# Two-layer kernel: order and size of loads at the borders of projection, scan and mix

## The chip, the cores and the metric

The kernel runs on one core of a Trainium2 chip. The metric is the device time of one execution in microseconds. TensorE multiplies matrices, VectorE and ScalarE do elementwise work, GpSimd does elementwise work and small tables, and SyncE (SP) issues DMAs; ScalarE issues some too. Each engine runs its own list of instructions in order, and semaphores tie the lists together.

## The reference

Two layers on x of 2 x 4096 tokens with 512 channels, all in float32. Biases are added where a matrix is applied. In the names of the kernel:

```
xn  = layernorm(x)
z   = silu(depthwise_conv3(xn @ w1.T + b1))             # over tokens
y   = ssm(z)         # h = h * sigmoid(A) + z * B; y = sum(h * C) + D * z, 16 states a channel
v   = silu(xn @ v1.T + bv1)
x2  = x + (y * v) @ w2.T + b2 + mxfp6(xn) @ mxfp6(Wf).T + bf
xn2 = layernorm(x2)
out = x2 + linear_attention_norm(xn2) + rwkv_channel_mix(xn2)
```

`mxfp6` scales blocks of 32 values by their largest magnitude over 7.5 and rounds to a grid of six-bit numbers. The recurrence of `ssm` runs over the 4096 tokens of a sequence; the kernel takes it in chunks of 16 tokens, with a small convolution inside a chunk and a scan from chunk to chunk. The linear attention needs sums over all tokens of a sequence of k, and of k times v, before its first output.

## The kernel before, in words

The first layer is one block of three phases that run into each other: `phase_project`, `phase_scan`, `phase_mix`. `run_phases` gives each engine the list of the three phases one after the other. The second layer follows in a block of its own. All orders are written out by hand.

**Projection.** 16 groups g of 512 tokens. VectorE normalises group g + 1 in `body(g)` (`normalise`, L285 to L302: statistics, rstd from GpSimd, then four scalings of 128x512). TensorE transposes it (`turn_x`, L486) between the products of group g, which are three products a piece (`split_products`, L99 to L101). ScalarE takes the x1 banks (L439) and the v banks (L452), and the centre tap of the convolution; VectorE adds the side taps (`side_terms`, L322 and L325), then takes the low part of the transposed x (`low_part`, L307), for which the turn of channel tile kt + 2 waits. VectorE also prepares tables of the scan at the end of a body: `state_rates` at g = 1 and 2, `state_powers` at g = 3 (four doublings, a last product, a copy, and a memset of `kpad`, L363), `kernel_rows` at g = 5. GpSimd raises the state matrix to powers by `power_bit(j)` behind the rstd of groups 4 to 7. SP stores z and v of each group; in the last group it stores v and z of channel tile 0, of tile 1, and of tiles 2 and 3. z of tile 0 of the last two units counts on `z_head`.

**Scan.** 64 steps o, eight channels each. SP loads z of a step into one of Z = 6 buffers (L592). TensorE makes three matmuls a step, of two passes each: `own` (L747) one step ahead, `toep` (L765), `outof` (L768). VectorE runs the recurrence (`scan`, L629) from `own` to `outof`. ScalarE takes y (L699) and stores it from one of Y = 4 buffers (L703). GpSimd expands three tables a step (L611). In between stand other jobs, by step number:

```
    TURN_AT, WEIGHTS_AT, QUANTISE_AT = 24, 32, 8
    MIX_IN_AT, MIX_PREPARE_AT, MIX_TURN_AT, MIX_HEAD_AT = 42, 44, 60, 61
```

VectorE quantises Wf in nine steps from QUANTISE_AT. ScalarE's queue loads Wf (`wf_nat`, 1 MB) before step 0 (L710), and at step 4 w2, Wk and Wv, 1 MB each, and three bias rows (L719 to L722). Two x tiles are normalised (`normalise_input`) and quantised (`prepare_step`, seven steps each; `finish_quantising` on GpSimd at 56 and 63); tile 0 is turned at 60.

**Mix.** 64 tiles N of 128 tokens, and pairs of tiles. Each tile takes a bank that ScalarE fills with the biases (`set_sums`, L996), quantised x times Wf and gated y times w2. VectorE adds x and takes statistics (`sums`, L1131), then ScalarE normalises and keys follow a tile or two later. The gated pair is `gate` (L1073, VectorE, once y and v are loaded), `high_u` (L974, ScalarE), `low_u` (L939, GpSimd). In iteration N, VectorE does `prepare_step(N + 2, ...)` and every second time a gate before `sums(N)`; GpSimd does `low_u` of the next pair after tile N's rstd when N is odd.

## Time and profile before

| | |
|---|---|
| median of 3 runs | 2188.6 us (2184.38 to 2189.14) |
| the profiled execution's own time | 2185.81 us |
| its span | 2184.0 us |
| mean granted TensorE clock | 0.986 |
| TensorE busy | 2108.4 us, 97% of the span |
| VectorE busy | 1509.2 us, 69% |
| ScalarE busy | 1058.5 us, 48% |
| GpSimd busy | 826.6 us, 38% |

Times within the trace count from the span's start. Busy time is what an engine's instructions take; a matmul's end is modelled, so that matmuls overlap in the record and their starts are what tells the pace. Idle time ahead of an instruction stands in brackets with what released it. The granted clock (PEclk) is TensorE's, 1.00 for its full 2.4 GHz.

### The profile page before, as it was taken

What the parts mean: (1) busy time and instruction counts of PE and PEld (TensorE: products, weight loads), DVE (VectorE), ACT (ScalarE), POOL (GpSimd) and SP (SyncE); (2) the same over time, 40 slices, a digit from 0 to 9 for tenths busy, and PEclk for the clock granted to TensorE, in tenths of its full rate; (3) what the DMA queues carried; (4) which work ended last, traced back from release to release, by engine and by line L of the source; (5) the groups of instructions that cost most, each with busy time, mean ns of one, the idle gap of its engine ahead of it and who ended that gap; (6) DMA issues with size and microseconds to landing.
All of it is one profiled execution on the core that took longest, in us unless ns stands there. A gap on an engine that the chain in (4) does not pass through costs nothing. (4 is left out here: it accounts for less than half of the span.)

```text
span 2184.0 us, 27599 instructions
## 1 busy us (share of the span) xinstructions
PE 2108.4 (97%) x9466; PEld 1671.5 (77%) x9466; DVE 1509.2 (69%) x2949; ACT 1058.5 (48%) x1770; POOL 826.6 (38%) x843
## 2 busy tenths in 40 slices
PE   7999999899899999999999999599999999999998
PEld 6878888534478888888888887478888888888887
DVE  4776655466577777776777774377777777777777
ACT  4545555323255555555555554355554444555443
POOL 1021000254445454444454453034434444443444
PEclk9999999999989999999999999799999999999999
DMA  4333533666533333332343331412222122222211
GB/s 148 125 112 133 162 121 107 237 216 211 183 106 126 97 116 117 106 116 97 118 143 106 108 125 49 145 49 87 85 80 68 68 68 87 87 85 80 68 39 39
DMA packets 173493, 241.38 MB, mean 111 GB/s; under 512 B 18857, under 2 KB 109225, under 8 KB 172202
## 3 DMA queue, kind: packets, MB, share of 16 engines
q1 hardware_dynamic: 161576, 216.10, 29.8%
q10 hardware_dynamic: 11778, 23.53, 2.9%
q8 instruction: 75, 1.23, 0.2%
q14 instruction: 64, 0.52, 0.1%
HBM read 138.86 MB, written 100.73 MB: 110 GB/s over the span
## 5 line engine op out<-in xcount | busy, mean ns | idle before, releaser
L99 PE MATMUL bank<-e_ring,e_w_hi 128*128 128x512 f32 x512 | 204.4, 399 | 22.2 <-DVE e_ring L1571 16.7
L1236 PE MATMUL bank<-d_kh,d_nat 128*128 128x512 f32 x768 | 196.0, 404 | 5.5 <-DVE d_kh L1122 5.5
L100 PE MATMUL bank<-e_ring,e_w_hi 128*128 128x512 f32 x512 | 200.6, 392 | 0.0
L101 PE MATMUL bank<-e_ring,e_w_lo 128*128 128x512 f32 x512 | 200.3, 391 | 0.0
L1571 DVE TENSOR_TENSOR e_ring<-e_mixed,e_ring 128x512 fp32r<-128x512 f32 x128 | 96.0, 750 | 122.6 <-ACT e_ring L1469 122.6
L1500 ACT ACTIVATE e_kr<-bank 128x512 f32<-128x512 f32 x64 | 38.0, 593 | 289.9 <-PE bank L101 233.0
L957 POOL TENSOR_TENSOR rstd<-d_var_eps,neg_half 128x1 f32<-128x1 f32 x64 | 35.3, 551 | 359.7 <-DVE d_var_eps L1142 359.7
L1236 PEld LDWEIGHTS bank<-d_kh,d_nat 128*128 128x128 f32 x768 | 141.3, 191 | 35.4 <-issue 6.5
L1450 POOL TENSOR_TENSOR e_x<-e_x,e_beta 128x512 f32<-128x512 f32 x64 | 82.9, 1295 | 223.8 <-ACT e_y L1491 223.8
L1430 POOL TENSOR_TENSOR e_x<-e_x,e_ff 128x512 f32<-128x512 f32 x64 | 83.2, 1301 | 196.3 <-DVE e_ff L1632 196.3
L247 POOL TENSOR_TENSOR b_rstd<-b_var_eps,neg_half 128x4 f32<-128x4 f32 x16 | 16.2, 1012 | 318.4 <-DVE b_var_eps L296 318.4
L99 PEld LDWEIGHTS bank<-e_ring,e_w_hi 128*128 128x128 f32 x512 | 96.7, 189 | 50.5 <-DVE e_ring L1571 18.9
L1021 ACT ACTIVATE d_xt<-bank 128x512 f32<-128x512 f32 x64 | 38.4, 599 | 190.8 <-PE bank L1199 190.8
L629 DVE TENSOR_TENSOR_SCAN c_state<-decay,bank 128x255 f32<-128x255 f32 x128 | 80.5, 670 | 71.4 <-PE bank L747 71.4
L1564 DVE SCALAR_TENSOR_TENSOR e_mixed<-e_xt,cols,e_prev 128x512 f32<-128x512 f32 x128 | 102.9, 804 | 20.3 <-ACT e_prev L1478 19.8
L307 DVE TENSOR_TENSOR b_xt<-bank,b_xt 128x512 fp32r<-128x512 f32 x64 | 44.0, 690 | 104.9 <-ACT b_xt L402 104.6
L101 PEld LDWEIGHTS bank<-e_ring,e_w_lo 128*128 128x128 f32 x512 | 96.8, 189 | 20.6
L1434 POOL TENSOR_TENSOR e_y<-e_y,e_att 128x512 f32<-128x512 f32 x64 | 107.0, 1671 | 14.3 <-DVE e_att L1651 14.3
L99 PE MATMUL bank<-d_w,d_ut 128*128 128x512 f32 x256 | 102.3, 400 | 10.1 <-POOL d_ut L939 5.6
L100 PEld LDWEIGHTS bank<-e_ring,e_w_hi 128*128 128x128 f32 x512 | 96.9, 189 | 18.8
L1147 DVE TENSOR_TENSOR d_nat<-d_xn,d_nat 128x512 fp32r<-128x512 f32 x64 | 78.2, 1222 | 47.2 <-ACT d_nat L1038 47.2
L99 PE MATMUL bank<-d_wk,d_nt 128*128 128x512 f32 x256 | 105.2, 411 | 0.0
(209 smaller groups left out, 6364.6 us busy)
## 6 DMA issues: line engine op xcount, KB each, us to landing
scr_v<-b_vt SPq DMA_DIRECT2D x64, 256.0 KB, 2.7
scr_z<-b_zt SPq DMA_DIRECT2D x64, 256.0 KB, 2.1
c_z<-scr_z SPq DMA_DIRECT2D x64, 256.0 KB, 2.7
scr_y<-c_y ACTq DMA_DIRECT2D x64, 256.0 KB, 2.7
d_x<-in_L_attn_x SPq DMA_DIRECT2D x64, 256.0 KB, 3.5
scr_x<-d_x SPq DMA_DIRECT2D x64, 256.0 KB, 2.1
scr_xnt<-d_xt SPq DMA_DIRECT2D x32, 512.0 KB, 4.0
e_xt<-scr_xnt SPq DMA_DIRECT2D x16, 1024.0 KB, 5.7
```

The lines of the kernel that those rows point to most:

```text
L99: eng.matmul(out, lhs[hi], rhs[hi], start=first, stop=False, skip_group_check=onto)
L100: eng.matmul(out, lhs[hi], rhs[lo], start=False, stop=False, skip_group_check=onto)
L101: return eng.matmul(out, lhs[lo], rhs[hi], start=False, stop=last, skip_group_check=onto)
L307: nc.vector.tensor_tensor(xt[g % 2][:, 1, kt, :], TB[kt % 2][:, :], xt[g % 2][:, 0, kt, :].bitcast(F32), ALU.subtract).then_inc(lo_done, 1)
L629: nc.vector.tensor_tensor_scan(state[o % 2][:, b, 1:], rate, SB[o % 2][:, b * NCB:(b + 1) * NCB - 1], 0.0, ALU.mult, ALU.add).then_inc(sta ...
L1147: nc.vector.tensor_tensor(nat[q][:, 1, :], xn[N % 2][:, :], nat[q][:, 0, :].bitcast(F32), ALU.subtract).then_inc(nat_lo, 1)
L1236: mm = pe.matmul(BG[c][:, :], s[:, i, cols], r[:, j, :], start=M % NTB == 0 and i == j, stop=M % NTB == NTB - 1 and i == 1, skip_group_che ...
L1430: nc.gpsimd.tensor_tensor(x2[h][:, t, :], x2[h][:, t, :], ff[t % 2][:, :], ALU.add).then_inc(base_done, 1)
L1434: nc.gpsimd.tensor_tensor(y[t][:, :], y[t][:, :], att[t % 2][:, :], ALU.add).then_inc(sum_done, 1)
L1450: nc.gpsimd.tensor_tensor(x2[h][:, t, :], x2[h][:, t, :], beta[:, :], ALU.add).then_inc(shifted, 1)
L1564: nc.vector.scalar_tensor_tensor(mixed[kt % 2][:, :], current(g % 2, kt), mu[:, kt:kt + 1], prev[kt % 2][:, :], ALU.mult, ALU.add).then_in ...
L1571: nc.vector.tensor_tensor(ring[slot][:, 1, kt, :], src, ring[slot][:, 0, kt, :].bitcast(F32), ALU.subtract).then_inc(lo_done, 1)
```

## The change

Where each load, table and tile stands in the engines' queues:

- Projection: `state_powers` is done in two parts, three doublings at g = 3 and the last with the rest at g = 4. The memset of `kpad` goes to GpSimd, ahead of everything. `kernel_rows`, its matmuls, and the store and the eight loads of the table go one group later. GpSimd's `power_bit` waits until its group has been normalised.
- SP loads the first six z blocks (`load_first_z`) behind the z stores of channel tile 1 of the last group, ahead of v and z of tiles 2 and 3.
- ScalarE's queue loads Wf in four pieces of 256 KB at steps 1 to 4, w2, Wk and Wv in twelve at every second step from 6 to 28, the bias rows at 30, 32 and 34. Quantising Wf starts at step 10, not 8. `join_biases` goes from step 24 to 42.
- Three x tiles, not two, are normalised and quantised in the scan, from step 38 and 40 on; tile 0 is turned at 56 and its high and low parts are taken at 57 and 58. In the mix, pair 1's `high_u` and `low_u` come ahead of tile 1, and iteration 0 quantises no tile.

```diff
@@ phase_project, sync
                     store_v(g, parts_v)
                     for c in units_in(g):
                         store_z(c, parts_z)
+                    if parts_z == (1,):
+                        keep["load_first_z"]()
                 continue
...
-            if g == 6:
+            if g == 7:
                 sp.wait_ge(k_step, 3)
...
-            if g == 7:
+            if g == 8:
                 sp.wait_ge(kern_out, 16)
@@ phase_project, gpsimd
+        nc.gpsimd.memset(kpad[:, :, :], 0.0).then_inc(keep["set"], 1)
...
             if g in (4, 5, 6, 7):
+                pool.wait_ge(xn_done, GT * (g + 1))
                 power_bit(g - 4)
@@ phase_project, vector
-        def state_powers():
-            for j in range(4):
+        def state_powers(doublings):
+            for j in doublings:
...
+            if 3 not in doublings:
+                return
...
-            nc.vector.memset(kpad[:, :, :], 0.0).then_inc(a_step, 1)
...
-            if g == 5:
+            if g == 6:
                 kernel_rows()
...
-            if g == 3:
-                state_powers()
+            if g in (3, 4):
+                state_powers(range(3) if g == 3 else (3,))
@@ phase_project, tensor
-            if g == 4:
+            if g == 5:
                 pe.wait_ge(a_step, 14)
@@ phase_scan
-    TURN_AT, WEIGHTS_AT, QUANTISE_AT = 24, 32, 8
-    MIX_IN_AT, MIX_PREPARE_AT, MIX_TURN_AT, MIX_HEAD_AT = 42, 44, 60, 61
+    TURN_AT, WEIGHTS_AT, QUANTISE_AT = 24, 32, 10
+    QUANTISED_AT, WEIGHT_PIECES_AT, BIASES_AT = 1, 6, 30
+    MIX_IN_AT, MIX_PREPARE_AT, MIX_BANKS_AT, MIX_TURN_AT, MIX_HEAD_AT = 38, 40, 42, 56, 61
+    MIX_FINISH_AT = {50: 0, 57: 1, NO - 1: 2}
...
+    def load_z(o):
+        nc.sync.dma_start(zo[o % Z][:, :], z_of[o]).then_inc(z_in[o % Z], 16)
+
+    def load_first_z():
+
+        nc.sync.wait_ge(*project["turned"])
+        nc.sync.wait_ge(*project["x1"])
+        nc.sync.wait_ge(*project["z_head"])
+        for h in range(2):
+            nc.sync.wait_ge(*project["z_front"][h])
+        for o in range(Z):
+            load_z(o)
...
@@ phase_scan, sync
+        project["store_last_v"]()
+        for o in range(Z, NO):
             if o == NO // KT:
                 for h in range(2):
                     sp.wait_ge(*project["z"][h])
-            if o >= Z:
-                sp.wait_ge(y_full, o - Z + 1)
-            sp.dma_start(zo[o % Z][:, :], z_of[o]).then_inc(z_in[o % Z], 16)
-            if o == 3:
-                project["store_last_v"]()
+            sp.wait_ge(y_full, o - Z + 1)
+            load_z(o)
@@ phase_scan, gpsimd
-            if o == 24:
+            if o == MIX_BANKS_AT:
                 mix["join_biases"]()
-            if o in (56, NO - 1):
-                mix["finish_quantising"](0 if o == 56 else 1)
+            if o in MIX_FINISH_AT:
+                mix["finish_quantising"](MIX_FINISH_AT[o])
@@ phase_scan, vector
-            if MIX_PREPARE_AT <= o < MIX_PREPARE_AT + 2 * mix["steps"]:
+            if MIX_PREPARE_AT <= o < MIX_PREPARE_AT + 3 * mix["steps"]:
                 mix["prepare_step"](*divmod(o - MIX_PREPARE_AT, mix["steps"]))
+            if o == MIX_TURN_AT + 2:
+                mix["low_q"](0)
...
-            if o == NO - 1:
-                mix["low_q"](0)
@@ phase_scan, scalar
-        act.dma_start(wf_nat[:, :].rearrange("p (t k) -> p t k", t=KT),
-                      ins["L0_ffn_weight"].rearrange("(t p) k -> p t k", p=P)).then_inc(wf_in, 16)
...
+            if QUANTISED_AT <= o < QUANTISED_AT + KT:
+                t = o - QUANTISED_AT
+                act.dma_start(wf_nat[:, t * D:(t + 1) * D], ins["L0_ffn_weight"][t * P:(t + 1) * P, :])\
+                   .then_inc(wf_in, 16)
...
-                act.dma_start(w2_raw[:, :, :], ins["L0_attn_w2_w"]).then_inc(raw_in[0], 16)
-                act.dma_start(wk_raw[:, :, :], ins["L1_attn_Wk"]).then_inc(raw_in[1], 16)
-                act.dma_start(wv[:, :, :], ins["L1_attn_Wv"]).then_inc(late["wv_in"], 16)
-                mix["load_biases"]()
+            if WEIGHT_PIECES_AT <= o < WEIGHT_PIECES_AT + 2 * 3 * KT and (o - WEIGHT_PIECES_AT) % 2 == 0:
+                i, kt = divmod((o - WEIGHT_PIECES_AT) // 2, KT)
+                tile, name, done = pieces[i]
+                act.dma_start(tile[:, kt, :], ins[name][:, kt, :]).then_inc(done, 16)
+            if o in (BIASES_AT, BIASES_AT + 2, BIASES_AT + 4):
+                mix["load_bias"]((o - BIASES_AT) // 2)
...
-            if o in (MIX_IN_AT, MIX_IN_AT + 1):
+            if MIX_IN_AT <= o < MIX_IN_AT + 3:
                 mix["normalise_input"](o - MIX_IN_AT)
...
-            if o == NO - 2:
+            if o == MIX_TURN_AT + 1:
                 mix["high_q"](0)
@@ phase_mix, gpsimd
-            if N % 2 and N // 2 + 1 < NT // 2:
+            if (N % 2 or N == 0) and N != 1 and N // 2 + 1 < NT // 2:
                 low_u(N // 2 + 1)
-            if N + 2 < NT:
+            if N and N + 2 < NT:
                 finish_quantising(N + 2)
@@ phase_mix, scalar
         high_u(0, BEHIND)
-        normalise_input(2)
+        high_u(1)
...
-            if N % 2 and N // 2 + 1 < NT // 2:
+            if N % 2 and N > 1 and N // 2 + 1 < NT // 2:
                 high_u(N // 2 + 1)
@@ phase_mix, vector
-            if N + 2 < NT:
+            if N and N + 2 < NT:
                 for k in range(PREP):
                     prepare_step(N + 2, k)
```

## Rows read from the trace of the kernel before

**Rows 1.** Timeline, ScalarE: start us, us, instruction, [idle before <- releaser].

```profile
114.78 0.69 ACT L439 ACTIVATE b_ring<-bank,cols 128x512 f32<-128x512 f32 x1 [1.08 <-PE bank L101]
...
146.49 0.69 ACT L439 ACTIVATE b_ring<-bank,cols 128x512 f32<-128x512 f32 x1 [3.08 <-PE bank L101]
...
170.18 0.69 ACT L439 ACTIVATE b_ring<-bank,cols 128x512 f32<-128x512 f32 x1 [1.06 <-PE bank L101]
```

**Rows 2.** Windows: busy us (instructions) of each engine, PEclk, DMA share, GB/s.

```profile
120.00:130.00 10.00, 6.95 (x30) 5.57 (x29) 8.83 (x16) 3.38 (x6) 7.00 (x4) 0.89 0.10 39
614.40:619.20 4.80, 4.78 (x11) 3.79 (x12) 4.59 (x8) 0.00 (x0) 2.62 (x2) 0.50 0.16 60
```

**Rows 3.** Timeline, VectorE, in the projection.

```profile
116.35 1.76 DVE L363 MEMSET b_kpad<- 8x2048 f32 x1 [0.36 <-issue]
...
123.96 4.66 DVE L302 TENSOR_SCALAR b_xg<-b_xg,b_moments,b_rstd 128x512 f32<-128x512 f32 x4
...
196.64 1.91 DVE L302 TENSOR_SCALAR b_xg<-b_xg,b_moments,b_rstd 128x512 f32<-128x512 f32 x4
...
206.28 0.68 DVE L307 TENSOR_TENSOR b_xt<-bank,b_xt 128x512 fp32r<-128x512 f32 x1
```

**Rows 4.** Timeline, TensorE, projection and scan.

```profile
210.96 0.60 PE L486 MATMUL bank<-consts,b_xg 128*128 128x128 f32 x4
...
410.13 3.78 PE L747 MATMUL bank<-c_z,c_into 128*128 128x512 f32 x4 [7.72 <-DMA c_z<-scr_z]
...
415.83 1.02 PE L747 MATMUL bank<-c_z,c_into 128*128 128x512 f32 x2
...
439.00 1.02 PE L747 MATMUL bank<-c_z,c_into 128*128 128x512 f32 x2
...
446.80 1.91 PE L747 MATMUL bank<-c_z,c_into 128*128 128x512 f32 x2
...
470.42 1.02 PE L747 MATMUL bank<-c_z,c_into 128*128 128x512 f32 x2
```

**Rows 5.** DMA issues (x, KB, us to landing): all; 403.6-404; 425-445; 592.3-592.7.

```profile
c_z<-scr_z SPq DMA_DIRECT2D x64, 256.0 KB, 2.7
...
c_z<-scr_z SPq DMA_DIRECT2D x1, 256.0 KB, 6.5
...
d_wv<-in_L_attn_Wv ACTq DMA_DIRECT2D x1, 1024.0 KB, 10.3
...
d_v<-scr_v SPq DMA_DIRECT2D x1, 512.0 KB, 4.6
```

**Rows 6.** Timeline, ScalarE, in the scan.

```profile
443.55 0.60 ACT L699 ACTIVATE c_y<-bank 128x512 f32<-128x512 f32 x1 [8.90 <-DMA scr_y<-c_y]
```

**Rows 7.** Timeline, TensorE, start of the mix.

```profile
601.29 0.80 PE L99 MATMUL bank<-d_w,d_ut 128*128 128x512 f32 x1 [4.47 <-ACT bank L996]
...
614.42 0.76 PE L99 MATMUL bank<-d_w,d_ut 128*128 128x512 f32 x1 [4.46 <-POOL d_ut L939]
...
625.94 0.39 PE L99 MATMUL bank<-d_w,d_ut 128*128 128x512 f32 x1
```

**Rows 8.** Timeline, SyncE, end of the projection.

```profile
396.22 0.91 SPq L213 DMA_DIRECT2D scr_z<-b_zt  x2
...
398.25 0.94 SPq L213 DMA_DIRECT2D scr_z<-b_zt  x2
```

**Rows 9.** Timeline, VectorE, start of the mix.

```profile
598.78 1.22 DVE L1073 TENSOR_TENSOR d_ut_raw<-d_ut_raw,d_v 128x1024 f32<-128x1024 f32 x1
599.92 0.68 DVE L1131 TENSOR_TENSOR d_x<-bank,d_x 128x512 f32<-128x512 f32 x1
```

**Rows 10.** Timeline, ScalarE, start of the mix.

```profile
604.94 1.04 ACT L974 ACTIVATE d_ut<-d_ut_raw 128x1024 fp32r<-128x1024 f32 x1
...
610.53 0.61 ACT L996 ACTIVATE bank<-d_res_bias 128x512 f32<-128x512 f32 x1
```

**Rows 11.** Timeline, GpSimd, start of the mix.

```profile
611.92 2.35 POOL L939 TENSOR_TENSOR d_ut<-d_ut_raw,d_ut 128x1024 fp32r<-128x1024 f32 x1
```

More of the change, by code:

```diff
@@ L362, in state_powers @@
             nc.vector.tensor_copy(keep["decay"][:, :], a_cs[:, 4, :]).then_inc(a_step, 1)
-            nc.vector.memset(kpad[:, :, :], 0.0).then_inc(a_step, 1)
         def kernel_rows():
-            dve.wait_ge(a_step, 17)
+            dve.wait_ge(a_step, 16)
+            dve.wait_ge(keep["set"], 2)
             for i in range(2):
@@ L577, in phase_scan @@
     }
-    def sync(sp):
-        sp.wait_ge(*project["turned"])
-        sp.wait_ge(*project["z_head"])
-        for h in range(2):
-            sp.wait_ge(*project["z_front"][h])
-        for o in range(NO):
-            if o == 3:
-                sp.wait_ge(*project["x1"])
+    def load_z(o):
[8 more added lines that the diff above has]
+            load_z(o)
+    keep["load_first_z"] = load_first_z
+    def sync(sp):
+        project["store_last_v"]()
+        for o in range(Z, NO):
             if o == NO // KT:
@@ L643, in quantise_step @@
         def quantise_step(k):
-            dve.wait_ge(wf_in, 16)
+            dve.wait_ge(wf_in, 16 * KT)
             if k:
@@ L706, in weight_high @@
             if kt == 0:
-                act.wait_ge(raw_in[i], 16)
+                act.wait_ge(raw_in[i], 16 * KT)
             nc.scalar.activation(tile[:, 0, kt, :], raw[:, kt, :], ACT.Copy).then_inc(w_hi, 1)
-        act.dma_start(wf_nat[:, :].rearrange("p (t k) -> p t k", t=KT),
-                      ins["L0_ffn_weight"].rearrange("(t p) k -> p t k", p=P)).then_inc(wf_in, 16)
+        pieces = [(w2_raw, "L0_attn_w2_w", raw_in[0]), (wk_raw, "L1_attn_Wk", raw_in[1]),
+                  (wv, "L1_attn_Wv", late["wv_in"])]
         for o in range(NO):
             take(o)
-            if o == 4:
+            if QUANTISED_AT <= o < QUANTISED_AT + KT:
+                t = o - QUANTISED_AT
+                act.dma_start(wf_nat[:, t * D:(t + 1) * D], ins["L0_ffn_weight"][t * P:(t + 1) * P, :])\
+                   .then_inc(wf_in, 16)
+            if o == WEIGHT_PIECES_AT:
                 for h in range(2):
@@ L730, in scalar @@
             store(o)
[L731 removed]
+            if MIX_IN_AT <= o < MIX_IN_AT + 3:
                 mix["normalise_input"](o - MIX_IN_AT)
[L733 removed]
+            if o == MIX_BANKS_AT + 6:
                 mix["set_sums"](0)
@@ L771, in tensor @@
                 turn_weight(o - TURN_AT)
-            if o == MIX_IN_AT:
+            if o == MIX_BANKS_AT:
                 mix["open_banks"]()
@@ L961, in gpsimd, with load_bias @@
                                         -1.0, ALU.mult, ALU.mult).then_inc(norm_done, 1)
-            if N % 2 and N // 2 + 1 < NT // 2:
+            if (N % 2 or N == 0) and N != 1 and N // 2 + 1 < NT // 2:
                 low_u(N // 2 + 1)
-            if N + 2 < NT:
+            if N and N + 2 < NT:
                 finish_quantising(N + 2)
-    def load_biases():
-        load_row(act, res_bias, ins["L0_attn_w2_b"]).then_inc(const_in, 16)
-        load_row(act, xn[1], ins["L0_ffn_bias"]).then_inc(const_in, 16)
-        load_row(act, bk, ins["L1_attn_bk"]).then_inc(const_in, 16)
+    def load_bias(i):
+        tile, name = ((res_bias, "L0_attn_w2_b"), (xn[1], "L0_ffn_bias"), (bk, "L1_attn_bk"))[i]
+        load_row(act, tile, ins[name]).then_inc(const_in, 16)
     def high_u(pair, parts=slice(0, KT)):
@@ L1157, in values @@
             dve.wait_ge(kv_full, b + 1)
-            dve.wait_ge(keep["set"], 2)
+            dve.wait_ge(keep["set"], 3)
             for j in range(HP):
@@ L1258, in sums_column @@
             mm.then_inc(kc_full, 1)
-        pe.wait_ge(late["wv_in"], 16)
+        pe.wait_ge(late["wv_in"], 16 * KT)
         pe.wait_ge(sums_set, 1 + B)
```

4 lines of the change are left out of this document (1 added, 3 removed).

## The prediction

> **What bounds the kernel now.** I read the stretches of the first layer first, then who waits for whom, then the order of time on each engine round every place where TensorE was idle. The reader is to see a TensorE that is never short of work except at three borders, and that pays twice for each stop: the idle time, and then a stretch at the lower clock.
>
> Stop 1 lies in the projection, group 4 to group 5. ScalarE takes the first x1 bank of each group. From group 5 to 6 this comes 170.18 - 146.49 = 23.69 us later, from group 4 to 5 it comes 31.71 us later [rows 1]. So 8.0 us are lost. In 120 to 130 us TensorE was busy for 6.95 us, idle for 3.05 [rows 2]; the other 5.0 us of the 8.0 are matmuls at the lower level (the two levels are 1.2 and 2.4 GHz; 0.50 granted in [rows 2] is the lower). What ends last there is `normalise` on VectorE: the memset of kpad at 116.35 stands ahead of it, and its four scalings take 4.66 us instead of 1.91 while GpSimd runs the power bits [rows 3].
>
> Stop 2 is the start of the scan. TensorE ends the projection at 410.13 - 7.72 = 402.41 and waits for the first z block; step 2 starts at 415.83 [rows 4]. That block is issued at about 403.6 and lands 6.5 us later, where the median load of this kind takes 2.7 [rows 5]. Just ahead of it or beside it are four last z stores and the 1 MB of `wf_nat`.
>
> Stop 3 is at steps 10 to 12 of the scan. A step takes (439.00 - 415.83) / 9 = 2.574 us, all of it TensorE at full clock. Ten steps from 415.83 should end at 441.57, but step 12 starts at 446.80: 5.2 us lost, and the next pair of matmuls takes 1.91 us instead of 1.02, 0.9 more [rows 4]. ScalarE waits 8.90 us there for a y store to land [rows 6], behind 3 MB of weights: the last megabyte landed after 10.3 us [rows 5].
>
> Stop 4 is the start of the mix. Its tiles 1 and 2 begin after 4.47 and 4.46 us of idle [rows 7], the second followed by 4.8 us at half clock [rows 2].
>
> **The change, part by part.** The sum is made against the profiled execution's own 2185.8 us (span 2184.0); the median of the runs is 2188.6, 2.8 above it.
>
> State powers. VectorE's queue ahead of the group's `normalise` loses the memset with the idle before it, 1.76 + 0.36 = 2.1 us [rows 3], and the last doubling. GpSimd's power bits now wait for `xn_done`, so the scalings go back from 4.66 to 1.91, 2.75 us. Together at least 4.8 us against the 3.05 that were missing: the stop goes, and with it the slow stretch. **-8.0 us.** The last doubling, a part of what leaves, stands one group later, where TensorE had no stop; kernel rows and the table's DMAs move by one group (23.7 us) and are needed only at the scan: nothing. The eight table loads then stand ahead of another group's x load on SP, as they did before, with no stop of TensorE: nothing. The memset on GpSimd runs before its first rstd, in time in which it has nothing to do: nothing.
>
> What GpSimd's wait moves is contention: the bits now start when `side_terms` does. Those take two SBUF inputs each. In group 7 the first `low_part` behind them starts at 206.28 and the transpose that needs it at 210.96 [rows 3, 4]; 4.68 - 0.68 = 4.0 us are spare. GpSimd's four instructions in that stretch are 7.00 us, one of them the rstd, which stays where it is [rows 2]; I put the other three at 6.0. Lower bound 0 (GpSimd is the one held up), upper bound 6.0 of delay, which beyond the 4.0 spare is 2.0 us in each of three groups, and some more in the one where kernel rows stand ahead of `low_part`. I take 0: of the 6.0 us only 2.75 came through to the scalings, and ScalarE, which feeds the side terms bank by bank, leaves gaps among them.
>
> The Trainium skill, SBUF — State Buffer, section Who interferes with whom, says that a VectorE instruction with two SBUF inputs and a GpSimd instruction that reads SBUF exclude each other for a whole instruction, the one that came first holding the other up. By that rule the side terms can be held for GpSimd's whole time, and the gain would be smaller by what rival (a) gives. The slowed scalings agree with a lock; no row here shows a side term under it.
>
> First z sooner. SP issues all six loads behind the z stores of channel tile 1, which are issued from 398.25 for 0.94 us [rows 8]. It first waits for the z stores of tile 0, issued until 397.13 [rows 8]; with 2.7 us for a block [rows 5] they have landed by 399.8. The first load lands 2.7 later, 402.5, against TensorE's 402.41. From there four pairs of matmuls, a third of a step each (0.86), lead to step 2 at 402.5 + 3.4 = 405.9, with no slow clock. Before: 415.83. **-9.8 us.** Bounds: 10.0 if the block is never waited for; 6 if it lands after 6.5 us again. Moved behind six issues on SP (about 4 us) are one v store and four z stores; their readers come at step 6 on ScalarE and at the load of block 16, over 15 us later: nothing. `wf_nat` in four pieces at steps 1 to 4 is first read at step 10, 15 us later: nothing.
>
> Weights in pieces. One piece of 256 KB every second step adds 128 KB to a step's 512. 3 MB and the biases came in at some 10.3 us for the last megabyte, about 300 KB per us, that is 770 KB in a step. So no y store is late by four steps (10.3 us), and the stop goes. **-6.1 us** (5.2 + 0.9). Bounds: 0 to 6.1. The extra issues on ScalarE's queue, at most one a step, stand beside a copy of 0.60 us in 2.57 [rows 6]: nothing. Quantising the weight comes two steps later with the same nine operations. Steps 12 to 20 take 470.42 - 446.80 = 23.62 us where eight steps are 20.6; 0.9 is counted above, about 2.1 are VectorE's quantising [rows 4], and stay.
>
> The Trainium skill, DMA: Bandwidth & Descriptors, section Bandwidth, advises transfers of 1 MiB and more; its fit of 2.0 us plus size at 436 GB/s is an estimate of 2.6 us for a piece. Were they run one after another, the sum would be some 49 us worse, which is the slow rival. The trace speaks against it: y stores that land in about 2.7 us follow each other every 2.57 us, with z loads of 2.7 us beside them [rows 5].
>
> Three x tiles in the scan. VectorE has seven more small steps, one in each step of the scan, where fourteen of the same run now without a stop of TensorE: nothing, and the same for GpSimd's third tile. Then the mix: v of pair 1 lands at 592.4 + 4.6 = 597.0 [rows 5], but its gate waited for `prepare_step` until 598.78 [rows 9]. After: gate 597.0 to 598.25, ScalarE's high copy (1.04, [rows 10]) to 599.3, the bank 0.6 more, so tile 1 starts at 600.0 instead of 601.29: -1.2. `low_u(1)` stood behind tile 1's statistics, at 611.92 for 2.35 us [rows 11]; it now follows tile 0's and is done some 8 us sooner. Tile 2 then waits only for its bank, set at 610.53 + 0.61 = 611.1 instead of 614.42 [rows 7, 10]: -3.3. The idle time is then about 1.2 us; so the 4.8 us at half speed should go, which hold 2.4 us of work: -2.4. VectorE now has quantising and a gate ahead of tile 2's sum, which tile 3 waits for: +0.8, my estimate from quantising and gate taking until about 618. Tile 3 starts at 619.8 instead of 625.94. **-6.1 us**; bounds -2 (the first stop stays, and so does the slow stretch) and -8. After tile 3 TensorE is full and keeps the gain. `low_q(0)` early gains 0.9 on paper but the last y block is waited for anyway: nothing.
>
> Sum: 8.0 + 9.8 + 6.1 + 6.1 = 30.0. 2185.8 - 30.0 = 2155.8, or 2158.6 on the median. I say 2157.
>
> **Rivals.** (a) Side terms held by GpSimd, as above: 3 x 2.0 us and kernel rows' part, 2157 + 7 = 2164. For it: the scalings in [rows 3]. Against: gaps among the side terms. (b) The mix border gives only part: ScalarE's high copy now stands ahead of the bank of tile 1 and waits for the gate and so for v; each us by which v lands later goes to TensorE, and a long idle time brings the slow stretch back. It gains 2: 2161. For it: that transfer is on the path with nothing to spare. (c) Slower: the pieces hold up ScalarE's queue of transfers. 4 + 12 + 3 = 19 pieces at 2.7 us each [rows 5] are 51 us, 2157 + 51 = 2208. It decides from 30 / 19 = 1.6 us a piece. Against: the overlap of y stores. (d) The z block lands after 6.5 us in spite of the order, since z stores are still ahead: gain 6 instead of 9.8, 2161.
>
> **Chances.** Forecast 0.66, (a) 0.12, (b) 0.12, (d) 0.07, (c) 0.03. Measurement of this kernel can tell about 0.2%, 4 us. (c) alone is slower, 0.03; 0.01 for no change, if parts of it meet the rest; faster 0.96. The range holds the forecast with 2151 (the mix bound -8, and the runs' own spread of 5 us) below, and above it (b), (d) and (a) with a few us: 2150 to 2167.
>
> **What would show it.** In the profile after: the first x1 banks of all groups 23.7 us apart; step 0 of the scan under 0.5 us after the projection's last matmul, step 2 at about 398 (8.0 + 9.8 earlier); steps 10 to 13 2.57 us each and ScalarE never waiting for a y store; quantising still losing about 2 us; tile 3 of the mix about 30 us earlier than 625.94. Side terms of over 1 us and a transpose that waits for `b_xt` would show (a). The prediction is wrong if TensorE has new idle time in the scan at every second step, or if a slow clock follows a stop that I hold to be short.

## The result and the profile after

The changed kernel takes 2161.22 us (median of 4 runs, 2159.82 to 2163.15), the kernel before 2187.01 us beside it (4 runs, 2184.38 to 2189.14). The ratio is 0.9884, 95% interval [0.9872, 0.9897]. The forecast of 2157 was 4 us too low; the range of 2150 to 2167 held it. The profiled execution has a span of 2161.1 us and a mean granted clock of 0.990, against 2184.0 and 0.986. That is 22.9 us, where the sum said 30.0. The medians differ by 25.8 us; the 3 us between the two differences lie in which executions were profiled, the slowest of four for the changed kernel (2163.15 us) and one below the median for the kernel before (2185.81 us). Where the 22.9 us lie is read off at six checkpoints, the same in both traces:

| stretch | before us | after us | gained | forecast |
|---|---|---|---|---|
| start to the first x1 bank | 20.01 | 20.82 | -0.8 | 0 |
| to the first bank of the last group | 363.41 | 357.40 | 6.0 | 8.0 |
| to step 2 of the scan | 32.41 | 22.61 | 9.8 | 9.8 |
| to step 22 | 59.74 | 54.21 | 5.5 | 6.1 |
| to step 63 | 108.38 | 108.42 | 0.0 | 0 |
| to tile 8 of the mix | 101.50 | 98.66 | 2.8 | 6.1 |
| to the end | 1498.5 | 1499.0 | -0.4 | 0 |

A "step" is the start of that step's `own` on TensorE; a tile starts with its first product of w2 there (L99, `d_ut`), tile 8 at 662.12 us. The first row is not the change: in the traces of all the kernels below this bank starts between 19.84 and 22.10 us.

**Projection.** ScalarE's first x1 banks (the timeline of the changed kernel), to be held against [rows 1]:

```profile
115.58 0.69 ACT L445 ACTIVATE b_ring<-bank,cols 128x512 f32<-128x512 f32 x1 [1.06 <-PE bank L101]
...
139.27 0.69 ACT L445 ACTIVATE b_ring<-bank,cols 128x512 f32<-128x512 f32 x1 [1.06 <-PE bank L101]
...
164.98 0.69 ACT L445 ACTIVATE b_ring<-bank,cols 128x512 f32<-128x512 f32 x1 [3.08 <-PE bank L101]
```

From 115.58 to 139.27 are 23.69 us: the stop is gone. But from 139.27 to 164.98 are 25.71, 2.0 more than the pace. TensorE shows what they are:

```profile
160.10 1.88 PE L523 MATMUL bank<-out_pow,consts 128*8 128x512 f32 x4
```

These are the four matmuls of the kernel rows. They went one group later, and before they stood inside the 31.71 us. Of the 8.0 us taken for a stop, 2.0 were work.

The window of 120 to 130 us (columns as in [rows 2]) has TensorE full at the full clock, where it had 6.95 us and 0.89:

```profile
120.00:130.00 10.00, 10.00 (x50) 8.29 (x49) 9.89 (x10) 4.91 (x8) 7.08 (x3) 1.00 0.24 91
```

In the same stretch VectorE (first fence) does the scalings and the side terms, and GpSimd (second) the power bit:

```profile
119.73 1.91 DVE L306 TENSOR_SCALAR b_xg<-b_xg,b_moments,b_rstd 128x512 f32<-128x512 f32 x4
...
122.33 2.27 DVE L329 SCALAR_TENSOR_TENSOR b_zt<-b_ring,cols,b_zt 128x512 f32<-128x512 f32 x1
124.52 0.75 DVE L326 SCALAR_TENSOR_TENSOR b_zt<-b_ring,cols,b_zt 128x512 f32<-128x512 f32 x1
125.31 1.42 DVE L329 SCALAR_TENSOR_TENSOR b_zt<-b_ring,cols,b_zt 128x512 f32<-128x512 f32 x1
126.65 2.89 DVE L326 SCALAR_TENSOR_TENSOR b_zt<-b_ring,cols,b_zt 128x512 f32<-128x512 f32 x1
```

```profile
121.72 2.33 POOL L256 TENSOR_TENSOR b_a_sq<-b_a_cr 128x1024 f32<-128x1024 f32 x1 [2.10 <-DVE b_xg L306]
124.16 2.03 POOL L259 TENSOR_SCALAR b_a_sel<-b_a_sq,consts 128x1024 f32<-128x1024 f32 x1
126.28 2.72 POOL L263 TENSOR_TENSOR into_t<-into_t,b_a_sel 128x1024 f32<-128x1024 f32 x1
```

The scalings are back at 1.91 us, as worked out from [rows 3]. The side terms are held: 2.27, 1.42 and 2.89 us where one takes 0.75 when it has the memory to itself, 4.3 us more in all. Each of the three ends 0.54 to 0.55 us after the GpSimd instruction that was under way (124.60 after 124.05). So the mechanism of rival (a) is there, in full size. Its price is not: TensorE has no wait in these groups. It is a near thing. Behind the side terms stands the low part of channel tile 0, for which the third transpose of the group waits (first fence VectorE, second TensorE):

```profile
131.69 1.28 DVE L311 TENSOR_TENSOR b_xt<-bank,b_xt 128x512 fp32r<-128x512 f32 x2
```

```profile
132.67 0.60 PE L492 MATMUL bank<-consts,b_xg 128*128 128x128 f32 x4
```

The first of the two low parts ends at about 132.4, 0.3 us before the transpose starts.

**Start of the scan.** SyncE issues the six loads from 394.19 on, and TensorE's `own` shows no idle time before step 0 and no slow clock from step 2 on (first fence SyncE, second TensorE):

```profile
394.19 2.78 SPq L588 DMA_DIRECT2D c_z<-scr_z  x6
```

```profile
397.06 2.22 PE L768 MATMUL bank<-c_z,c_into 128*128 128x512 f32 x4
...
400.83 1.02 PE L768 MATMUL bank<-c_z,c_into 128*128 128x512 f32 x2
...
426.58 0.59 PE L768 MATMUL bank<-c_z,c_into 128*128 128x512 f32 x1
...
437.32 1.10 PE L768 MATMUL bank<-c_z,c_into 128*128 128x512 f32 x2 [0.27 <-issue]
...
452.39 1.10 PE L768 MATMUL bank<-c_z,c_into 128*128 128x512 f32 x2 [0.89 <-issue]
455.04 1.02 PE L768 MATMUL bank<-c_z,c_into 128*128 128x512 f32 x2
```

The block that step 0 needs was there within 397.06 - 394.19 = 2.9 us of its issue; in [rows 4] step 0 had waited 7.72 us. Steps 2 to 12 (400.83 to 426.58) take 25.75 us, ten times 2.575: no step is late while the weights come in pieces. What still loses are the steps with quantising, those that start at 437.32 and 452.39 among them.

**Mix.** TensorE's waits there, to be held against [rows 7]:

```profile
575.01 0.50 PE L99 MATMUL bank<-d_w,d_ut 128*128 128x512 f32 x1 [2.29 <-POOL d_ut L960]
...
579.85 0.79 PE L99 MATMUL bank<-d_w,d_ut 128*128 128x512 f32 x1 [3.44 <-ACT bank L1016]
...
589.27 0.50 PE L99 MATMUL bank<-d_w,d_ut 128*128 128x512 f32 x1 [1.23 <-ACT bank L1016]
...
598.97 0.50 PE L99 MATMUL bank<-d_w,d_ut 128*128 128x512 f32 x1 [0.30 <-ACT bank L1016]
...
612.99 0.47 PE L99 MATMUL bank<-d_w,d_ut 128*128 128x512 f32 x1 [1.88 <-POOL d_ut L960]
```

These are tiles 0 to 4. Tile 1 still starts behind 3.44 us of idle time, 4.47 before, with a slow clock behind it in both kernels. Counted from step 63, tile 3 starts at 35.51 us (598.97 - 563.46) and before at 41.99: 6.5 gained, 6.1 forecast. Then comes a wait that before did not have: tile 4, 1.88 us, for GpSimd. GpSimd's own rows:

```profile
609.62 0.55 POOL L978 TENSOR_TENSOR rstd<-d_var_eps,neg_half 128x1 f32<-128x1 f32 x1 [5.13 <-DVE d_var_eps L1162]
...
610.49 2.36 POOL L960 TENSOR_TENSOR d_ut<-d_ut_raw,d_ut 128x1024 fp32r<-128x1024 f32 x1
```

`low_u(2)`, the low part of pair 2, stands behind tile 3's rstd and so behind VectorE's statistics of tile 3, which GpSimd waits 5.13 us for. ScalarE's high part of the pair is there from 604.90 + 1.04 = 605.9 on. It is the same order of the queue that had held tile 2 before [rows 11]; the change took it away for pair 1 alone, and the wait came back one pair later. Behind it the clock falls:

```profile
612.90:617.00 4.10, 4.01 (x12) 3.19 (x13) 3.65 (x6) 1.41 (x3) 3.92 (x3) 0.64 0.00 0
```

4.1 us at 0.64 of the full clock are 1.5 us lost. So 6.5 - 1.9 - 1.5 = 3.1 are left, and 2.8 measured at tile 8; from tile 5 on (626.58 us) both kernels take 11.85 us a tile.

### The profile page after: what moved, and what is told of

It is laid out like the page before. It is cut to its first block and busy times, and to the rows that moved or that the text cites. A ratio compares the mean times of both kernels' runs of the same rounds, so it can differ in the third digit from the quotient of the medians.

```text
span 2161.1 us, 27615 instructions
## 1 busy us (share of the span) xinstructions
PE 2101.1 (97%) x9466; PEld 1668.3 (77%) x9466; DVE 1504.6 (70%) x2948; ACT 1057.1 (49%) x1770; POOL 828.8 (38%) x844
## 5 line engine op out<-in xcount | busy, mean ns | idle before, releaser
L99 PE MATMUL bank<-e_ring,e_w_hi 128*128 128x512 f32 x512 | 204.7, 400 | 22.2 <-DVE e_ring L1591 16.6
L99 PEld LDWEIGHTS bank<-e_ring,e_w_hi 128*128 128x128 f32 x512 | 96.9, 189 | 50.9 <-DVE e_ring L1591 18.9
L99 PE MATMUL bank<-d_w,d_ut 128*128 128x512 f32 x256 | 101.7, 397 | 9.1 <-ACT bank L1016 5.0
L99 PE MATMUL bank<-d_wk,d_nt 128*128 128x512 f32 x256 | 105.5, 412 | 0.0
```

The source lines that it names most:

```text
L99: eng.matmul(out, lhs[hi], rhs[hi], start=first, stop=False, skip_group_check=onto)
```

## The experiments

**One part alone.** Four kernels put one part of the change each into the kernel before. The fifth part, w2, Wk and Wv in twelve spread pieces, was not run alone.

First the state powers with the memset, the kernel rows' group and GpSimd's wait:

```diff
-                state_powers()
+            if g in (3, 4):
+                state_powers(range(3) if g == 3 else (3,))
...
+                pool.wait_ge(xn_done, GT * (g + 1))
                 power_bit(g - 4)
```

> The kernel before with the projection's part alone (state powers in two parts, kpad's memset on GpSimd, kernel rows a group later, power bits behind the group's normalise). The prediction's sum says 8.0 us less at the start of the scan. The rival, read from the trace of the changed kernel: the 8.0 us of the stop held some 2.0 us of kernel rows' own four matmuls, which only move to the next group, so the gain is 6.0 us: the x1 banks come 23.7 us apart from group 4 to 5, and 25.7 us apart from 5 to 6. VectorE's side terms are held up to 2.9 us by GpSimd in three groups, without a wait of TensorE in either theory.

2182.3 us; ratio 0.9982 [0.9973, 0.9991]; span 2177.8, 6.2 less than before. The medians differ by 4.0 us only, since this profiled execution was one of the faster of its eleven. The first banks of the groups are 23.69 and then 25.72 us apart, as in the changed kernel. Against the trace of before the term is 6, alone as in the whole.

Then only the order of the z loads; Wf is still one transfer of 1 MB, the weights three:

```diff
+                    if parts_z == (1,):
+                        keep["load_first_z"]()
```

> The kernel before with only the six first z loads ahead of the last v and z stores; wf_nat stays one load of 1 MB before step 0. If the order is what counts, step 2 of the scan starts 9.8 us earlier, as in the changed kernel. If the megabyte of wf_nat is what made the first z load take 6.5 us, it will still delay later z blocks (it is issued at about 402.5, when two to four of the six are on their way): TensorE waits for z1 to z3 some 1 to 4 us and the gain is 6 to 9 us. Total: 6 to 10 us faster.

2175.53 us; 0.9956 [0.9942, 0.9971]; span 2172.3, 11.7 less. From the first bank of the last group to step 2 it takes 22.49 us, 9.9 less than before, the whole term, though `wf_nat` stands where it stood. The other 1.8 us are no one term: the stop at group 5 was 2.7 us shorter in this execution (28.96 in place of 31.71), with no edit near it, so that the first term too can be 3 or 6 us from one execution to another, and at stop 3 1.6 were lost again. Steps 2 to 12 took 32.59 us in place of 30.97, the weights meeting the y stores in the same way (ScalarE's timeline):

```profile
431.29 0.60 ACT L708 ACTIVATE c_y<-bank 128x512 f32<-128x512 f32 x1 [9.54 <-DMA scr_y<-c_y]
```

Then only Wf in four pieces at steps 1 to 4:

```diff
-        act.dma_start(wf_nat[:, :].rearrange("p (t k) -> p t k", t=KT),
-                      ins["L0_ffn_weight"].rearrange("(t p) k -> p t k", p=P)).then_inc(wf_in, 16)
...
+            if 1 <= o < 1 + KT:
+                t = o - 1
+                act.dma_start(wf_nat[:, t * D:(t + 1) * D], ins["L0_ffn_weight"][t * P:(t + 1) * P, :])\
+                   .then_inc(wf_in, 16)
```

> The kernel before with only wf_nat cut into four pieces at steps 1 to 4 of the scan; the z loads stay behind all stores, at 403.6. If the megabyte made the first z load slow, z0 lands about 2.7 to 3.5 us after its issue, at 406.3 to 407.1 instead of 410.1, and 3 to 4 us are gained. If the z stores just ahead of it were the cause, it still lands after 5 us or more and 0 to 1.5 us are gained.

2183.39 us; 0.9991 [0.9982, 1.0001], which can't be told from no change; span 2179.9. TensorE waits for the first z block still, but for less (TensorE's timeline, to be held against the first row of [rows 4]):

```profile
406.92 2.94 PE L749 MATMUL bank<-c_z,c_into 128*128 128x512 f32 x4 [4.40 <-DMA c_z<-scr_z]
...
412.18 1.02 PE L749 MATMUL bank<-c_z,c_into 128*128 128x512 f32 x2
```

Step 2 comes 3.75 us sooner from the last group's bank, and 2.6 are given back at steps 2 to 12 (33.58 us). The last of the four pieces goes out in the same step as the 3 MB of weights, which is a likely cause and not tested; y stores issued from 420 to 445 us land after 12.7 us in the median, 11.5 before. Of the 4.1 us of the span, 2.2 lie behind step 63, with no edit near. The two ways to shorten stop 2 don't add: with the order changed there is nothing left for the size of Wf to gain.

Then only the third tile and the mix's order:

```diff
-    MIX_IN_AT, MIX_PREPARE_AT, MIX_TURN_AT, MIX_HEAD_AT = 42, 44, 60, 61
+    MIX_IN_AT, MIX_PREPARE_AT, MIX_BANKS_AT, MIX_TURN_AT, MIX_HEAD_AT = 38, 40, 42, 56, 61
...
-            if N % 2 and N // 2 + 1 < NT // 2:
+            if (N % 2 or N == 0) and N != 1 and N // 2 + 1 < NT // 2:
                 low_u(N // 2 + 1)
```

> The kernel before with only the third x tile in the scan and the reordering at the start of the mix. The prediction says 6.1 us by tile 3 and all of it kept. The rival, from the trace of the changed kernel: tile 3 starts 6 us earlier against the scan's end, but tile 4 then waits about 1.9 us for low_u of pair 2 on GpSimd, a stretch at the lower clock follows, and 2.5 to 3 us remain from tile 5 on and at the end.

2181.14 us; 0.9978 [0.9969, 0.9987]; span 2179.7, 4.3 less. Tile 8 starts 97.88 us after step 63, 3.6 sooner than before. The wait of tile 4 is here too (1.83 us), but no slow clock after it. So the order of the mix gives 3.6 without that stretch, not 6.1.

The four spans' gains are 6.2 + 11.7 + 4.1 + 4.3 = 26.3 us, against 22.9 of the whole. By the medians of the runs they are 4.0 + 10.7 + 2.9 + 5.1 = 22.7 us, against 25.8. With the fifth part missing, which the checkpoints credit with 5.5 us, and single executions this far apart, the sums say nothing on whether the parts add up. What each part is worth is read from its own stretch.

**The weights' pieces, all issued at step 6.** What does the spreading do, and what does the size do?

```diff
-            if WEIGHT_PIECES_AT <= o < WEIGHT_PIECES_AT + 2 * 3 * KT and (o - WEIGHT_PIECES_AT) % 2 == 0:
-                i, kt = divmod((o - WEIGHT_PIECES_AT) // 2, KT)
-                tile, name, done = pieces[i]
-                act.dma_start(tile[:, kt, :], ins[name][:, kt, :]).then_inc(done, 16)
+            if o == WEIGHT_PIECES_AT:
+                for n in range(3 * KT):
+                    i, kt = divmod(n, KT)
+                    tile, name, done = pieces[i]
+                    act.dma_start(tile[:, kt, :], ins[name][:, kt, :]).then_inc(done, 16)
```

> The changed kernel, but all twelve weight pieces of 256 KB are issued at once at step 6 of the scan. If it is the spacing that frees the y stores, the stop of the kernel before is back: ScalarE waits 5 to 9 us for a y store, TensorE 3 to 4 us with a slow clock behind it, 4 to 6 us slower than the changed kernel at step 20 (twelve issues at 0.35 to 0.45 us on ScalarE's queue add 4 us of delay to its copies too). If it is the size of a piece, there is no stop beyond those issues.

2167.57 us in its one run; span 2165.4, 4.3 more than the changed kernel. Steps 2 to 22 take 58.70 us, not 54.21: 4.5 of the 5.5 us are lost again. TensorE waits for ScalarE once (its timeline), step 10 to 11:

```profile
426.32 1.69 PE L787 MATMUL bank<-c_z,c_toep 128*128 128x512 f32 x2 [2.52 <-ACT c_y L714]
```

ScalarE's own timeline tells why:

```profile
417.99 1.79 ACTq L742 DMA_DIRECT2D d_w_raw<-in_L_attn_w_w  x4
...
422.38 2.67 ACTq L742 DMA_DIRECT2D d_wv<-in_L_attn_Wv  x4
...
425.67 0.60 ACT L714 ACTIVATE c_y<-bank 128x512 f32<-128x512 f32 x1 [7.24 <-issue]
...
432.69 0.60 ACT L714 ACTIVATE c_y<-bank 128x512 f32<-128x512 f32 x1 [2.33 <-DMA scr_y<-c_y]
```

From 417.99 to 425.05 ScalarE issues twelve transfers, 0.59 us each, and takes no y; TensorE, at 426.32, waits for the y that ScalarE takes at 425.67. ScalarE waits for a y store to land once, later on, 2.33 us where it was 8.90 in [rows 6], and TensorE has no wait there. So the 4.5 us are not the stop of the kernel before. They are the price of twelve issues in one step of the engine that also takes y. Whether the size of a piece or the spreading is what frees the y stores, this run doesn't separate; it shows that the spreading keeps the issues off TensorE's path.

**Without GpSimd's wait.** The changed kernel, the power bits back in their old place behind the rstd:

```diff
-                pool.wait_ge(xn_done, GT * (g + 1))
                 power_bit(g - 4)
```

> The changed kernel without GpSimd's wait for xn_done ahead of the power bits. The prediction counts the wait as 2.75 us of the 4.8 us it frees, of which 3.05 were missing; the memset and the last doubling alone free about 3.3. So the normalise of group 5 ends about 4.5 us later than in the changed kernel (121.6 to about 126) and just meets TensorE, which needs it at about 126.4: 0 to 0.5 us slower. If the scalings' slowing is what made the stop, TensorE waits 1 us or more there, with 2 to 5 us of slow clock. The side terms are then free of GpSimd (0.75 us each).

2160.46 us in its one run; span 2158.7. The first fence is VectorE, the second GpSimd:

```profile
118.62 1.85 DVE L303 COPY rstd<-b_rstd 128x4 f32<-128x4 f32 x1 [1.05 <-POOL b_rstd L249]
120.39 4.73 DVE L305 TENSOR_SCALAR b_xg<-b_xg,b_moments,b_rstd 128x512 f32<-128x512 f32 x4
125.05 0.74 DVE L325 SCALAR_TENSOR_TENSOR b_zt<-b_ring,cols,b_zt 128x512 f32<-128x512 f32 x1
```

```profile
118.56 1.90 POOL L256 TENSOR_TENSOR b_a_sq<-b_a_cr 128x1024 f32<-128x1024 f32 x1
120.56 1.74 POOL L259 TENSOR_SCALAR b_a_sel<-b_a_sq,consts 128x1024 f32<-128x1024 f32 x1
```

The scalings are slow again (4.73 us), even a copy of 128x4 is held 1.85 us, the side terms are free (0.74), and the groups are 23.72 us apart: no stop. Either engine may be the one that is held, for the same 4 us, and neither costs TensorE anything once the memset and the last doubling are gone. The wait that the change adds is worth nothing. The 2.4 us of span less are 1.0 at the start, 0.2 up to step 63, 0.8 up to tile 8, where this execution has no slow stretch, and 0.4 behind it: none is at the power bits.

**`low_u` ahead of the wait.** In each iteration of the mix, GpSimd's low part of the next pair stands before the wait for the tile's statistics:

```diff
-            if (N % 2 or N == 0) and N != 1 and N // 2 + 1 < NT // 2:
-                low_u(N // 2 + 1)
+            if N == 0:
+                low_u(1)
...
                 add_keys(N - 3)
+            if N % 2 and N != 1 and N // 2 + 1 < NT // 2:
+                low_u(N // 2 + 1)
             if N < NT:
                 pool.wait_ge(stat, 3 * N + 3)
```

> The changed kernel with GpSimd's low_u of the next pair ahead of the rstd of an odd tile, instead of behind it (from tile 3 on). Theory: the mix gives back 3.5 us at tile 4 because low_u of pair 2 stands behind tile 3's statistics; then TensorE no longer waits for it, the slow stretch behind it goes, and this is 2.5 to 3.5 us faster than the changed kernel, tile 8 about 26.5 us ahead of the kernel before. Rival: the rstd of odd tiles comes 2.4 us later and with it the normalised x and the keys; TensorE then waits elsewhere and the time is the same or worse.

2159.5 us; 0.9877 [0.986, 0.9893]; span 2157.7, 3.4 less than the changed kernel. GpSimd:

```profile
605.96 2.39 POOL L960 TENSOR_TENSOR d_ut<-d_ut_raw,d_ut 128x1024 fp32r<-128x1024 f32 x1 [1.51 <-ACT d_ut L996]
```

It runs 4.5 us sooner, as soon as ScalarE's high part is there. As the rival had it, tile 3's rstd comes later, by 1.9 us counted from step 63, but TensorE doesn't wait for it. TensorE's wait at tile 4 is gone, and so is the slow stretch: 1.9 + 1.5 = 3.4 us. TensorE's row of tile 8 says the same, 658.63 - 563.63 = 95.00 us after step 63 where the changed kernel takes 98.66, 3.7 less:

```profile
658.63 0.39 PE L99 MATMUL bank<-d_w,d_ut 128*128 128x512 f32 x1
```

The queue's order was the cause of the wait. The 1.5 us of slow clock can't be put down to the order in the same way, since other kernels have the wait without it (below). The ratio alone, 0.9877 against 0.9884, doesn't tell this kernel from the changed one.

**Why quantising costs.** Steps 2 to 25 of the changed kernel take 61.93 us, where 23 steps of 2.574 are 59.2. I first held that VectorE had not enough slack with long operations in steps on end, and spread them out:

```diff
-    TURN_AT, WEIGHTS_AT, QUANTISE_AT = 24, 32, 10
+    TURN_AT, WEIGHTS_AT, QUANTISE_AT = 24, 32, (7, 8, 9, 10, 12, 13, 14, 17, 20)
...
-            if QUANTISE_AT <= o < QUANTISE_AT + 9:
-                quantise_step(o - QUANTISE_AT)
+            if o in QUANTISE_AT:
+                quantise_step(QUANTISE_AT.index(o))
```

> The changed kernel with the nine steps of quantising Wf at steps 7, 8, 9, 10, 12, 13, 14, 17 and 20 of the scan instead of 10 to 18, so that no two of the five long ones (2.3 to 2.4 us) follow each other. Theory: the 2.7 us that TensorE loses in steps 14 to 22 are three long steps in a row on VectorE, whose lag adds up; spread, each lag of 0.9 us stays under the slack of about 1.2 us: 2.0 to 2.7 us faster. Rival: part of the loss is the DMA traffic of the pieces or the clock; then under 1 us.

2163.59 us in its one run; span 2160.7. Steps 2 to 25 take 61.25 us: 0.7 gained, where the theory wanted nearly all. A single long operation, with room on both sides, still costs 0.5 us. The theory fell. The timelines of the changed kernel, read again, first VectorE and then GpSimd, show another engine that is late:

```profile
433.97 2.27 DVE L669 TENSOR_TENSOR c_wf_nat<-c_wf_nat,c_q_inv 128x2048 f32<-128x2048 f32 x1
```

```profile
434.56 1.94 POOL L626 TENSOR_TENSOR c_into<-into_t,consts 128x128 f32<-128x128 f32 x1 [1.46 <-PE bank L789]
436.46 0.40 POOL L626 TENSOR_TENSOR c_toep<-toep_t,consts 128x128 f32<-128x128 f32 x1
436.82 0.40 POOL L626 TENSOR_TENSOR c_outof<-out_pow,consts 128x128 f32<-128x128 f32 x1
```

A table that GpSimd expands in 0.40 us takes 1.94 when it meets VectorE's operation with two inputs, and ends 0.26 us after it. Beside VectorE's operation of one input at 437.32 (1.34 us, L671) a table takes 1.38, so that it is not the two inputs alone. `own` waits for all three tables of its step (436.82 + 0.40 = 437.22), and starts at 437.32 with idle time before it. It was tested from both ends. With a fourth buffer for each table:

```diff
-    Z, Y, TABS = 6, 4, 3
+    Z, Y, TABS = 6, 4, 4
```

> The changed kernel with four buffers for each of GpSimd's three tables of a scan step instead of three, so that GpSimd may be one step further ahead. It asks why quantising Wf costs TensorE about 2.7 us. In the changed kernel steps 2 to 25 of the scan take 61.93 us (23 steps of 2.574 would be 59.2). Theory G: what is late at a quantising step is not VectorE's own recurrence but GpSimd's tables; in the traces so far a table of 0.40 us takes 1.94 when VectorE's 128x2048 operation with two inputs runs, and ends just when that one ends, and own waits for all three tables of its step. With 2.57 us more of lead, steps 2 to 25 take 59.2 to 59.8 us. Theory V: VectorE's recurrence behind an operation of 2.3 us is what is late; the tables' lead changes nothing, 61.9 as before. The whole: G 2158.5, V 2161.

2159.88 us in its one run; span 2158.0. Steps 2 to 25 take 60.46 us: 1.5 of the 2.7 us are gone, at the steps where only tables were late. Step 41 to 42 takes 0.5 us longer, though, and the steps from 25 to 63 together 0.4 (101.09 in place of 100.70), so that the buffer is worth 1.1 in all; why is open. The other 1.2 stay, and are now put down to VectorE's recurrence (TensorE's timeline):

```profile
448.88 1.13 PE L789 MATMUL bank<-c_state,c_outof 128*128 128x512 f32 x2
...
452.36 1.12 PE L789 MATMUL bank<-c_state,c_outof 128*128 128x512 f32 x2 [0.65 <-DVE c_state L644]
```

So both theories hold, for a part each. And with the same work in slices of 512 columns:

```diff
+        def sliced(out, a, b, op):
+            for s in range(4):
+                at = slice(s * NB // 4, (s + 1) * NB // 4)
+                nc.vector.tensor_tensor(out[:, at, :], a[:, at, :], b[:, at, :], op).then_inc(q_step, 1)
...
-                ins_ = nc.vector.tensor_tensor(blocks, blocks, wide(q_inv), ALU.mult)
+                ins_ = sliced(blocks, blocks, wide(q_inv), ALU.mult)
```

> The changed kernel with the four two-input operations of quantising (128x2048, 2.27 us each) cut into four of 128x512 each, in the same steps. Theory G with a hold that lasts one instruction: GpSimd's tables get in between the slices, each table takes at most 0.4 + 0.6 = 1.0 us instead of 1.94, but three in a row may each be held once, 3.0 us in place of 1.94 + 0.8 = 2.7, so that the gain is small or none: steps 2 to 25 of the scan 61.0 to 62.2 us; what decides is how long one table takes, 1.0 or less. Theory G with a hold that lasts as long as VectorE has such work at hand: the first table still takes 1.9 or more. Theory V: VectorE's time grows by some 0.2 us in each of four steps, steps 2 to 25 take 62.5 us or more and the tables' times say nothing.

2159.95 us in its one run; span 2158.2. First VectorE, then GpSimd:

```profile
432.77 2.88 DVE L663 TENSOR_TENSOR c_wf_nat<-c_wf_nat,c_q_inv 128x512 f32<-128x512 f32 x4
```

```profile
433.36 0.94 POOL L626 TENSOR_TENSOR c_into<-into_t,consts 128x128 f32<-128x128 f32 x1 [1.46 <-PE bank L797]
434.26 0.84 POOL L626 TENSOR_TENSOR c_toep<-toep_t,consts 128x128 f32<-128x128 f32 x1
435.07 0.85 POOL L626 TENSOR_TENSOR c_outof<-out_pow,consts 128x128 f32<-128x128 f32 x1
```

No table is held for more than one slice: 0.94 us at most in place of 1.94. But now each of the three is held once, and VectorE itself takes 2.88 us where it took 2.27. Steps 2 to 25 take 62.40 us, 0.5 more than in the changed kernel. The hold is one instruction long, and slicing gains nothing when as many instructions of the other engine stand in the way.

**What is found, together.** The changed kernel with `low_u` first, no wait of the power bits, and four table buffers, and beside it the changed kernel once more:

> The changed kernel with three of the findings together: GpSimd's low part of the next pair ahead of its waits in an iteration of the mix, no wait of the power bits for the normalised group, and four buffers for each table of the scan. If the gains of the single runs hold side by side (2.4 and 3.4 us of span, of which about 1.5 of each is the slow stretch at tile 4 of the mix that only the changed kernel had, and 2.4 for the tables): span 2161.1 - 1.5 - 1.0 - 1.9 - 2.4 = 2154.3, median about 2155. Rival: each only moves a wait to the next engine in the queue, and the time stays at that of the low part alone, 2158 to 2160.

> The changed kernel once more, on the chip of the other three, so that they are compared with it there. Median 2161, span 2161. If the wait of 1.88 us at tile 4 of the mix is not followed by a stretch at the lower clock this time, span 2159.5; then that stretch was chance and not a part of the change.

The three together: 2157.22 us (4 runs, 2156.3 to 2158.58), ratio to before 0.9866 [0.9847, 0.9885], span 2155.2. The changed kernel: 2161.72 us (4 runs, 2161.16 to 2162.39), 0.9888 [0.9872, 0.9903], span 2159.9. The two medians are 4.5 us apart and their runs don't overlap. In the spans, steps 2 to 25 give 1.5 (60.45 in place of 61.93 us), steps 25 to 63 lose 0.4 again (101.08 in place of 100.69), and step 63 to tile 8 gives 3.6 (94.76 in place of 98.32); the start was alike. The spans had been expected at 2154.3 and 2161, or 2159.5 without the slow stretch.

The changed kernel's second trace has the slow stretch behind tile 4 again, so that "chance" is too simple a word for it. The wait of 1.83 to 1.88 us is there in eight traces of seven kernels; TensorE's clock falls behind it in two traces, both of the unaltered changed kernel, and stays at 1.00 in the six others, as here in the one with four tables and the one with slices:

```profile
611.70:616.70 5.00, 4.96 (x22) 4.15 (x23) 4.50 (x7) 1.36 (x3) 3.89 (x3) 1.00 0.00 0
```

```profile
612.70:617.00 4.30, 4.23 (x19) 3.53 (x20) 3.84 (x6) 1.39 (x3) 3.93 (x3) 1.00 0.00 0
```

The instructions ahead are the same in kind and order, at times that differ by tenths of a microsecond. What decides it stays open.

## Why the prediction was right, and where it was off

**Stop 1, 8.0 us forecast, 6.0 measured.** The mechanism was right: one kernel with this part alone gives the same 6. The mis-sized term is the difference of two periods. It took 31.71 - 23.69 as loss, but the group with 31.71 also had the four matmuls of the kernel rows, 1.88 us at L523, which are moved and not removed. They stand in the code at `if g == 4`, and the diff moves them; a list of what the long period holds would have found them. The reading that 5.0 us of the 8.0 were matmuls at the lower level falls with it: 3.05 were idle, 2.0 were this work, and about 3.0 are left for the slow clock. The bound (a) of held side terms, 0 to 2.0 us a group, was taken at 0, and 0 it was, though the reason given was wrong. I expected gaps among the side terms; they were held for 4.3 us, and what covered it was the slack ahead of the transposes, of which 0.3 us were left. That (a) cost nothing was luck by so much. The Trainium skill, SBUF — State Buffer, section Who interferes with whom, says that the instruction that comes second is shut out for the whole of the first: the side term of 2.89 us and the table of 1.94 us agree. By that rule the size of the hold was right and the price wrong, since that section says nothing of who waits for the one held. And of the two steps that were to add to 4.8 us, the removal from VectorE's queue was enough by itself: without GpSimd's wait the groups are 23.72 us apart.

**Stop 2, 9.8 and 9.8.** The block came in time, there was no slow clock, and the order alone gives 9.9. That Wf played a part in the 6.5 us was left open, and it did: in pieces alone, 3.75.

**Stop 3, 6.1 and 5.5.** Steps 2 to 12 run at full pace, and ScalarE waits for no y store in the whole scan; this is 5.2 of it and exact, and the 0.9 us of slow matmuls are gone too. What is missing, 0.6, is quantising, which was to stay at 2.1 us and takes 2.7. The two steps by which it was moved, priced at nothing, brought it beside another job of GpSimd (its timeline in the changed kernel):

```profile
448.56 0.98 POOL L950 MEMSET d_kacc<- 128x512 f32 x2
449.50 2.07 POOL L626 TENSOR_TENSOR c_into<-into_t,consts 128x128 f32<-128x128 f32 x1
```

The memsets of step 20 now stand ahead of the table that the last long operation holds, and step 21 starts 3.71 us after step 20; before, they came behind it (468.73 us), and its step took 3.13. No run tests this alone. The trace of before had the cause in its rows, unread: tables of 1.9 to 2.4 us on GpSimd beside VectorE's operations with two inputs. The fourth buffer gives 1.5 us back there.

**The third tile, 6.1 and 2.8.** This is the step that failed in size: "After tile 3 TensorE is full and keeps the gain". Up to tile 3 the working held (6.5). It then did not ask what `low_u(2)` waits for, although the sum of the same paragraph rests on `low_u(1)` having stood in that place. The order that costs 4.46 us at tile 2 is left for pair 2, and costs 1.88 at tile 4, with a slow stretch of 1.5. Moved ahead of the wait it costs nothing. The likeness to rival (b) is in the amount alone: the high copy and v did not come late in the way that it supposed, and tile 1 starts 0.95 us sooner counted from step 63, of the 1.2 forecast.

**The slow rival (c)** fell plainly: the pieces came in beside y stores, landing after 4.6 to 5.6 us in the median, and ScalarE waited for none of the stores. **(d)** did not occur: the first block took at most 2.9 us.

Summed in spans: 30.0 - 2.0 (work taken for loss) - 0.6 (quantising) - 3.3 (tile 4 and its clock) = 24.1; the start of this execution took 0.8 and the stretch behind tile 8 0.4 more, which makes 22.9, the difference measured.

That the forecast of the time is off by only 4 us, where the sum of the spans is off by 7, is partly luck: the executions that were profiled lie 3 us to the unfavourable side of the medians. Of the signs that the prediction named, the banks 23.7 us apart fail once (25.71), step 2 comes at 400.83 and not at 398, and tile 3 27.0 us earlier and not 30. A slow clock behind a short stop, which was to show the prediction wrong, did come, at tile 4, where it had no stop at all.

## What to carry to other kernels

A period that is too long is not all idle time: list the instructions in it that its neighbours don't have, and subtract those that the change only moves. When a queue's order causes a wait and is mended for one instance, look at the next instance of the loop before the gain is booked to the end. Where two engines share a way to memory, the one that is held need not be the one that costs: follow who waits for it, and give lead (a buffer more) to the one with a reader close behind. A transfer also costs its issue on the engine that sends it: twelve in a row are a job of 7 us.

## What the runs showed of the hardware

- VectorE and GpSimd hold each other up by whole instructions, either way round: a table of 128x128 on GpSimd 1.94 us instead of 0.40, a side term on VectorE 2.89 instead of 0.75, a copy of 128x4 1.85 instead of 0.17. Of VectorE's operations of one input, the one that only reduces 128x2048 (2.26 us) held no table, and the elementwise one (1.34 us) made one take 1.38.
- The same wait at the same place (1.83 to 1.88 us over all) is followed by the lower clock in two traces and by the full clock in six.
- 3 MB in twelve pieces cost nothing when one goes out every 5.1 us, and 4.5 us when ScalarE issues all in a row (7.06 us, 0.59 each), because TensorE waits for the y that ScalarE takes behind them.
